# Register loads of TensorE from a multiple of four words on, and one column value per tile in the flow stage

## The chip, the cores and the metric

The kernel runs on one core of a Trainium2 chip. The metric is the device time of one execution in microseconds (us); lower is better. A core has five engines that each follow their own instruction stream and meet through semaphores: TensorE (PE, matrix products), VectorE (DVE), ScalarE (ACT), GpSimd (POOL) and SyncE (SP). TensorE has a sequencer (shown as PEq or PEldq) that reads the stream, carries out register work itself and hands the matrix instructions on.

## The reference, cut to what matters

Four layers over a graph of 3125 nodes with 32 features and 53125 edges, each on a normalised `h` and added to `x`:

```python
h = relu(layernorm(x)); x = x + relational(relational(h))   # twice: sum over edges of a message by source and edge type
h = relu(layernorm(x)); x = x + segment_sum(h[src], dst, N) # sum layer
h = relu(layernorm(x)); x = x + flow(h, src, dst, edge_attr) # small MLP per edge, summed forward and backward
h = relu(layernorm(x)); x = x + attention(h, src, dst)       # softmax over the edges of a node, 4 heads
```

Each layer needs, for every edge, a row of its source node, and adds a result to the sum of its destination node.

## The kernel before

The edges are first sorted by block of destination: a node block holds 128 nodes (`NB` = 25 blocks), and every tile of 128 edges has destinations in one block only. There are `T` = 440 tiles. The sums of all nodes lie in PSUM as 25 column ranges of 32, so to add a tile, TensorE multiplies a one-hot of the destinations with the messages and writes to columns `col` to `col` + 32, where `col` is the tile's block times 32. These 440 column values lie as int32 words in one row of SBUF, `dst_columns` (`s["dcol"]`); TensorE's sequencer loads them into registers with `pe.load`, and `pe.snap` makes a value of a register that an address can use.

**Relational stages (rel1, rel2; `add_up_pass`).** A group is 11 tiles, 40 groups a stage. For 8 tiles of a group, POOL gathers the message rows with 8 indirect DMAs (L726, six buffers). For the other 3 tiles TensorE picks the source rows itself: DVE makes one-hots of the sources, one 128x384 comparison for each of the 25 blocks (L789, two buffers `which`), and TensorE runs 25 matmuls over them (`pick`, L863). Per group TensorE's stream is: `pick(g)`, `gathered_messages(g)` (8 sums, which wait for POOL's DMAs), `coefficients(g)`, `picked_messages(g-2)`, `basis_products(g)`. `pick(g)` begins with the load of the group's 11 column values (L858), and behind it in the stream comes the wait for `which_ready`.

**Sum stage (`sum_layer`).** Again 11 tiles a group and 40 groups; 7 tiles are gathered by POOL (L1029, four buffers), 4 are picked (25 comparisons of 128x512 at L1063, 25 matmuls at L1115). The load is L1110, at the head of `pick`; the order is `pick(g+1)`, `turn(g)`, `picked_rows(g-1)`, `gathered_rows(g)`.

**Flow stage (`flow_layer`).** A group is 4 tiles, 110 groups. `pick_destinations` loads 4 column values (L1379) and runs 12 small matmuls that read at the column; `add_up`, two groups later, runs 12 sums into the column and 24 into the backward accumulator. The two are interleaved by `step`. Each use calls `col(b, t)`, which snaps the register again (L1369). The attention stage has its own load of 8 words (L1767).

SP brings in the source rows; ACT moves picked results from PSUM to SBUF.

Of the kernel before, what the change touches and what calls it, by code (L numbers as in the profile page):

```python
# [19 lines left out]
F = 32  # L20
# [5 lines left out]
NB = (N + P - 1) // P  # L26
# [8 lines left out]
G = 8  # L35
# [35 lines left out]
def stages(rounds):  # L71

    def stage(function, i, k, behind, *more):
        i, k = i + (k - behind) // BUFS, (k - behind) % BUFS
        if not isinstance(i, int) or 0 <= i < rounds:
            function(i, i * BUFS + k, k, *more)
    return stage

def top(x):
# [543 lines left out]
RG, RPT, RBUFS = 11, 3, 6  # L625
# [48 lines left out]
def add_up_pass(nc, a, s, d, sb, ps, sem, k, init, finish):  # L674
# [3 lines left out]
    name = f"rel{k}"  # L678
    with ExitStack() as st:
        acc = ps(st, f"{name}_acc", [P, 2 * BANK])  # L680
        parts = init(st, acc)
        with ExitStack() as st1:
# [28 lines left out]
            with nc.Block() as block:  # L711
# [133 lines left out]
                @block.tensor  # L845
                def _(pe):
                    if k == 1:
                        edges["pe"](pe)
                    parts["pe"](pe)
                    regs = [[pe.alloc_register(f"{name}_col{i}{t}") for t in range(RG)] for i in range(3)]  # L850

                    def add(g, t, rhs):
                        col = pe.snap(regs[g % 3][t], min_val=0, max_val=(NB - 1) * F)
                        return pe.matmul(acc[:, bass.ds(col, F)], hot[g % RBUFS][:, t, :], rhs,
                                         start=False, stop=True, skip_group_check=True)

                    def pick(g):
                        pe.load(regs[g % 3], s["dcol"][0:1, 0, g * RG:(g + 1) * RG])  # L858
                        pe.wait_ge(which_ready, g + 1)
                        if g >= 2:  # L860
                            pe.wait_ge(pick_taken, g - 1)
                        for c in range(NB):
                            last = pe.matmul(pp[g % 2][0:3 * F, 0:RW], hs[:, c].rearrange("p k f -> p (k f)"),  # L863
                                             which[g % 2][:, c, :], start=(c == 0), stop=(c == NB - 1))
                        last.then_inc(pick_done, 1)

                    def gathered_messages(g):
                        b = g % RBUFS
                        pe.wait_ge(hot_ready, g + 1)
                        pe.wait_ge(gathered[b], 16 * RGT * (g // RBUFS) + 16 * RGT)  # L870
                        for t in range(RGT):
                            last = add(g, t, rows[b][:, t, :])
                        last.then_inc(rows_used, 1)

                    def coefficients(g):
                        pe.wait_ge(kinds_ready, g + 1)
                        if g >= 1:
                            pe.wait_ge(coef_taken, g)
                        for t in range(RPT):
                            last = pe.matmul(pc[:, t * NBASIS:(t + 1) * NBASIS], kinds[g % 2][:, t * P:(t + 1) * P],  # L880
                                             ab[:], start=True, stop=True)
                        last.then_inc(coef_done, 1)

                    def basis_products(g):
                        pe.wait_ge(pick_taken, g + 1)
                        if g >= 1:
                            pe.wait_ge(z_taken, g)
                        for t in range(RPT):
                            for j in range(3):
                                last = pe.matmul(pz[:, t * NBASIS * F:(t + 1) * NBASIS * F],  # L890
                                                 gT[g % 2][:, t * P:(t + 1) * P], top(V[:])[:, j, :],
                                                 start=(j == 0), stop=(j == 2))
                        last.then_inc(z_done, 1)

                    def picked_messages(g):
                        pe.wait_ge(msg_ready, g + 1)
                        for t in range(RPT):
                            last = add(g, RGT + t, msg[g % 2][:, t, :])
                        last.then_inc(used, 1)

                    for g in range(RGROUPS):
                        pick(g)
                        gathered_messages(g)
                        coefficients(g)
                        if g >= 2:
                            picked_messages(g - 2)
                        basis_products(g)
                    picked_messages(RGROUPS - 2)
                    picked_messages(RGROUPS - 1)
# [79 lines left out]
def sum_layer(nc, a, s, d, sb, ps, sem, more):  # L989
# [3 lines left out]
    G, PT, bufs = 11, 4, 4  # L993
# [3 lines left out]
    with ExitStack() as st:  # L997
# [5 lines left out]
        with ExitStack() as st2:  # L1003
# [16 lines left out]
            with nc.Block() as block:  # L1020
# [76 lines left out]
                def _(pe):  # L1097
                    pe.wait_ge(zeroed, 2)
                    clear_acc(pe, s, zeros, [acc[:, 0:BANK], acc[:, BANK:2 * BANK]])
                    regs = [[pe.alloc_register(f"sum_col{i}{t}") for t in range(G)] for i in range(3)]  # L1100

                    def add(g, t, hot, rhs):
                        col = pe.snap(regs[g % 3][t], min_val=0, max_val=(NB - 1) * F)
# [3 lines left out]
                        return last  # L1107

                    def pick(g):
                        pe.load(regs[g % 3], s["dcol"][0:1, 0, g * G:(g + 1) * G])  # L1110
                        pe.wait_ge(which_ready, g + 1)
                        if g >= 2:
                            pe.wait_ge(pick_taken, g - 1)
                        for c in range(NB):
                            last = pe.matmul(pp[g % 2][0:3 * F, 0:PT * P], hs[:, c].rearrange("p k f -> p (k f)"),  # L1115
                                             which[g % 2][:, c, :], start=(c == 0), stop=(c == NB - 1))
                        last.then_inc(pick_done, 1)
# [116 lines left out]
def flow_layer(nc, a, s, d, sb, ps, sem, front):  # L1234

    G = 4
    rounds = T // G // BUFS
    stage = stages(rounds)
    with ExitStack() as st:  # L1240
# [6 lines left out]
        with ExitStack() as st2:  # L1247
# [22 lines left out]
            with nc.Block() as block:  # L1270
# [94 lines left out]
                def _(pe):  # L1365
                    regs = [[pe.alloc_register(f"flow_col{b}{t}") for t in range(G)] for b in range(BUFS)]

                    def col(b, t):
                        return pe.snap(regs[b][t], min_val=0, max_val=(NB - 1) * F)  # L1369

                    def turn_onehots(i, g, b):
                        pe.wait_ge(hot_ready, g + 1)
# [4 lines left out]
                    def pick_destinations(i, g, b, products):  # L1377
                        if products[0] == 0:
                            pe.load(regs[b], s["dcol"][0:1, 0, bass.ds(g * G, G)])  # L1379
                            pe.wait_ge(ot_copied, g + 1)  # L1380
                        for n in products:
                            t, k = divmod(n, 3)
                            last = pe.matmul(pQ[:, t * F:(t + 1) * F], OT[:, t, :],
                                             top(hpart[:])[:, k, bass.ds(col(b, t), F)], start=(k == 0), stop=(k == 2))
                        if products[-1] == 3 * G - 1:
                            last.then_inc(q_done, 1)

# [20 lines left out]
                    def add_up(i, g, b, products):  # L1408
                        if products[0] == 0:
                            pe.wait_ge(msg_ready, g + 1)  # L1410
                        for n in products:
                            t, k = divmod(n, 3)
                            pe.matmul(accF[:, bass.ds(col(b, t), F)], hot[b][:, t, :], top(M[b][:])[:, k, t, 0:F],  # L1413
                                      start=False, stop=True, skip_group_check=True)
                            for lo, hi in ((0, BANK), (BANK, QJ)):
                                last = pe.matmul(accB[:, lo:hi], S[b][:, t, k, :],  # L1416
# [534 lines left out]
```

## Time and profile before

| | us |
|---|---|
| median of 3 runs | 3631.74 (3630.74 to 3633.47) |
| profiled execution, span of its records | 3621.4 |
| rel1, first to last register load of its groups | 648.3 to 1075.0 |
| rel2, the same | 1164.3 to 1597.2 |
| sum, the same | 1632.7 to 2010.4 |
| flow, the same | 2040.9 to 2856.3 |

The stages follow each other, with a barrier of all engines between them: what a stage gains moves all later ones. PE is busy 72% of the span, DVE 71%, POOL 62%; which of them sets the pace differs from stage to stage. All times below count from the start of the span. The median lies 10.3 us above the span; the difference is taken as fixed.

### The profile page before, as it was taken

What the parts mean: (1) busy time and instruction counts of PE and PEld (TensorE: products, weight loads), DVE (VectorE), ACT (ScalarE), POOL (GpSimd) and SP (SyncE); (2) the same over time, 40 slices, a digit from 0 to 9 for tenths busy, and PEclk for the clock granted to TensorE, in tenths of its full rate; (3) what the DMA queues carried; (4) which work ended last, traced back from release to release, by engine and by line L of the source; (5) the groups of instructions that cost most, each with busy time, mean ns of one, the idle gap of its engine ahead of it and who ended that gap; (6) DMA issues with size and microseconds to landing.
All of it is one profiled execution on the core that took longest, in us unless ns stands there. A gap on an engine that the chain in (4) does not pass through costs nothing. (4 is left out here: it accounts for less than half of the span.)

```text
span 3621.4 us, 58407 instructions
## 1 busy us (share of the span) xinstructions
PE 2609.3 (72%) x19499; PEld 1755.0 (48%) x19499; DVE 2555.5 (71%) x7445; ACT 577.7 (16%) x1352; POOL 2259.7 (62%) x2253
## 2 busy tenths in 40 slices
PE   0600000999998999977889799999999967777751
PEld 0400000777776777764555466666666543333331
DVE  9400000998874988869999677777777559999987
ACT  0100000000001000000011122222222213333320
POOL 2777776877762777747777355555555357777750
PEclk9555555788885888878889799999999968888885
DMA  6300001111113111111111100000000011111120
GB/s 96 103 8 8 8 8 58 31 23 24 25 12 103 25 23 24 24 17 28 26 27 26 12 10 10 11 10 10 10 11 10 6 24 27 27 27 27 27 19 5
DMA packets 125028, 91.67 MB, mean 25 GB/s; under 512 B 59542, under 2 KB 110678, under 8 KB 124118
## 3 DMA queue, kind: packets, MB, share of 16 engines
q0 software_dynamic: 70912, 41.10, 7.7%
q1 hardware_dynamic: 53846, 46.89, 5.3%
q8 instruction: 178, 2.92, 0.3%
q14 instruction: 92, 0.75, 0.1%
HBM read 60.42 MB, written 27.41 MB: 24 GB/s over the span
## 5 line engine op out<-in xcount | busy, mean ns | idle before, releaser
L726 POOL DMA_INDIRECT rel_rows<-message_table,message_indices x640 | 684.8, 1070 | 285.3 <-issue 193.9
L1279 POOL DMA_INDIRECT flow_x<-node_table,flow_index x440 | 441.0, 1002 | 409.8 <-DVE flow_index L1294 300.8
L1416 PE MATMUL flow_acc_bwd<-flow_onehot_j,flow_by_q 128*128 128x512 bf16 x2640 | 573.2, 336 | 0.0
L789 DVE TENSOR_SCALAR rel_source_onehot<-rel_sources,node_numbers 128x384 bf16<-128x384 f16 x2000 | 511.1, 320 | 79.4 <-PE p_rel_picked L863 78.0
L387 POOL DMA_INDIRECT sorted_edges<-stage,sorted_row x416 | 405.0, 974 | 192.0 <-issue 126.6
L863 PE MATMUL p_rel_picked<-rel_source_onehot,rel_h_parts 128*96 128x384 bf16 x2000 | 483.2, 417 | 53.7 <-issue 53.3
L1644 POOL DMA_INDIRECT att_kv_rows<-kv_table,att_index x440 | 427.1, 971 | 141.1 <-issue 131.7
L863 PEld LDWEIGHTS p_rel_picked<-rel_source_onehot,rel_h_parts 128*96 128x96 bf16 x2000 | 315.0, 161 | 214.2 <-issue 69.7
L1029 POOL DMA_INDIRECT sum_rows<-node_table,src_indices x280 | 272.1, 972 | 103.1 <-issue 80.8
L658 PE MATMUL p_rel_terms<-ident,source_centred 128*128 128x128 f32 (+1 forms) x4 | 1.1, 434 | 454.4 <-DVE source_centred L644 454.4
L1063 DVE TENSOR_SCALAR sum_source_onehot<-sum_sources,node_numbers 128x512 bf16<-128x512 f16 x1000 | 305.6, 371 | 14.9 <-PE p_sum_picked L1115 14.7
L755 DVE COPY p_rel_lanes<-iota 128x128 f32<-128x128 f32 x2 | 0.6, 294 | 438.8 <-PEq L382 436.2
L1680 DVE TENSOR_REDUCE att_tile_max<-p_att_scores 128x4 f32<-128x512 f32 x440 | 284.3, 685 | 28.0 <-PE p_att_scores L1794 23.1
L1115 PE MATMUL p_sum_picked<-sum_source_onehot,sum_h_stack 128*96 128x512 bf16 x1000 | 257.7, 421 | 51.4 <-issue 40.0
L1792 PE MATMUL p_att_scores<-att_mask,identb 128*128 128x512 bf16 x440 | 201.4, 458 | 67.2 <-ACT att_parts_turned L1728 67.2
L1413 PE MATMUL flow_acc_fwd<-flow_messages,flow_onehot 128*128 128x32 bf16 x1320 | 234.8, 178 | 1.4 <-DVE flow_by_q L1322 1.4
L838 ACT CAST rel_picked<-p_rel_picked 96x384 bf16<-96x384 f32 x80 | 38.0, 475 | 1171.6 <-PE p_rel_picked L863 1171.6
L658 PEld LDWEIGHTS p_rel_terms<-ident,source_centred 128*128 128x128 f32 (+1 forms) x4 | 0.7, 202 | 455.8 <-DVE source_centred L644 455.8
L1307 DVE TENSOR_TENSOR flow_messages<-p_hidden,flow_b 128x256 f32<-128x256 f32 x110 | 46.7, 425 | 245.9 <-PE p_hidden L1404 245.9
L1115 PEld LDWEIGHTS p_sum_picked<-sum_source_onehot,sum_h_stack 128*96 128x96 bf16 x1000 | 133.4, 137 | 162.6 <-issue 80.6
L1322 DVE TENSOR_TENSOR flow_by_q<-flow_messages,source_q_mask 128x512 bf16<-128x512 bf16 x330 | 207.4, 682 | 0.0
L1794 PE MATMUL p_att_scores<-att_parts_turned,att_pick 96*128 96x512 bf16 x440 | 205.7, 467 | 0.0
(286 smaller groups left out, 4882.9 us busy)
## 6 DMA issues: line engine op xcount, KB each, us to landing
message_table<-message_rows SPq DMA_DIRECT2D x50, 320.0 KB, 2.2
rel_rows<-message_table,message_indices POOLq DMA_INDIRECT x640, 2.5
rel_sources<-source_rows SPq DMA_DIRECT2D x80, 96.0 KB
flow_x<-node_table,flow_index POOLq DMA_INDIRECT x440
att_kv_rows<-kv_table,att_index POOLq DMA_INDIRECT x440, 2.4
sorted_edges<-stage,sorted_row POOLq DMA_INDIRECT x416
sum_sources<-source_rows SPq DMA_DIRECT2D x40, 128.0 KB, 3.0
sum_rows<-node_table,src_indices POOLq DMA_INDIRECT x280, 2.3
```

The lines of the kernel that those rows point to most:

```text
L387: pool.indirect_dma_start(out=d["sorted"], out_offset=bass.IndirectOffsetOnAxis(ap=row[:, c:c + 1], axis=0), in_=stage[:, c, :], in_offset ...
L726: pool.indirect_dma_start(out=rows[b][:, t, :], out_offset=None, in_=d["messages"], in_offset=bass.IndirectOffsetOnAxis(ap=s["idx_msg"][:, ...
L789: last = dve.tensor_scalar(which[g % 2][:, c, :], srcs[b][:], s["node"][:, c:c + 1], None, ALU.is_equal)
L863: last = pe.matmul(pp[g % 2][0:3 * F, 0:RW], hs[:, c].rearrange("p k f -> p (k f)"), which[g % 2][:, c, :], start=(c == 0), stop=(c == NB ...
L1029: pool.indirect_dma_start(out=rows[b][:, t, :], out_offset=None, in_=d["nodes"], in_offset=bass.IndirectOffsetOnAxis(ap=s["idx_src"][:, g ...
L1063: last = dve.tensor_scalar(which[g % 2][:, c, :], srcs[g % bufs][:], node[:, c:c + 1], None, ALU.is_equal)
L1115: last = pe.matmul(pp[g % 2][0:3 * F, 0:PT * P], hs[:, c].rearrange("p k f -> p (k f)"), which[g % 2][:, c, :], start=(c == 0), stop=(c == ...
L1279: pool.indirect_dma_start(out=X[b][:, t, 0:F], out_offset=None, in_=d["nodes"], in_offset=bass.IndirectOffsetOnAxis(ap=ibuf[b][:, t:t + 1] ...
L1413: pe.matmul(accF[:, bass.ds(col(b, t), F)], hot[b][:, t, :], top(M[b][:])[:, k, t, 0:F], start=False, stop=True, skip_group_check=True)
L1416: last = pe.matmul(accB[:, lo:hi], S[b][:, t, k, :], J[b][:, t, lo:hi], start=False, stop=True, skip_group_check=True)
L1644: pool.indirect_dma_start(out=KV[b][:, t, :], out_offset=None, in_=d["kv"], in_offset=bass.IndirectOffsetOnAxis(ap=ibuf[b][:, t:t + 1], ax ...
L1680: dve.tensor_reduce(tm[b][:, 0, t, :], pR[t % PR][:].rearrange("p (h e) -> p h e", h=HEADS), AX_X, ALU.max).then_inc(max_ready, 1)
```

## The change

A helper begins a load at the multiple of four words at or below the first word wanted; the 0 to 3 words ahead of it go into registers that nobody reads. It is used in the two relational stages and the sum stage, where a group's first word is 11g, so that the remainder of 4 runs 0, 3, 2, 1 and the lengths are 11, 14, 13, 12 words. In flow the snap is made once per tile, at the first of its three picks, and the value is kept in a dictionary for the other two picks and the three sums. No array operation is added or removed, and the other engines' streams are the same.

```diff
+def load_aligned(eng, unused, regs, table, first):
+
+    before = first % 4
+    eng.load(unused[0:before] + regs, table[:, first - before:first + len(regs)])
...
                     regs = [[pe.alloc_register(f"{name}_col{i}{t}") for t in range(RG)] for i in range(3)]
+                    unused = [pe.alloc_register(f"{name}_unused{i}") for i in range(3)]
...
-                        pe.load(regs[g % 3], s["dcol"][0:1, 0, g * RG:(g + 1) * RG])
+                        load_aligned(pe, unused, regs[g % 3], s["dcol"][0:1, 0, :], g * RG)
...
                     regs = [[pe.alloc_register(f"sum_col{i}{t}") for t in range(G)] for i in range(3)]
+                    unused = [pe.alloc_register(f"sum_unused{i}") for i in range(3)]
...
-                        pe.load(regs[g % 3], s["dcol"][0:1, 0, g * G:(g + 1) * G])
+                        load_aligned(pe, unused, regs[g % 3], s["dcol"][0:1, 0, :], g * G)
...
-                    def col(b, t):
-                        return pe.snap(regs[b][t], min_val=0, max_val=(NB - 1) * F)
+                    cols = {}
...
                             t, k = divmod(n, 3)
+                            if k == 0:
+                                cols[b, t] = pe.snap(regs[b][t], min_val=0, max_val=(NB - 1) * F)
                             last = pe.matmul(pQ[:, t * F:(t + 1) * F], OT[:, t, :],
-                                             top(hpart[:])[:, k, bass.ds(col(b, t), F)], start=(k == 0), stop=(k == 2))
+                                             top(hpart[:])[:, k, bass.ds(cols[b, t], F)], start=(k == 0), stop=(k == 2))
...
-                            pe.matmul(accF[:, bass.ds(col(b, t), F)], hot[b][:, t, :], top(M[b][:])[:, k, t, 0:F],
+                            pe.matmul(accF[:, bass.ds(cols[b, t], F)], hot[b][:, t, :], top(M[b][:])[:, k, t, 0:F],
                                       start=False, stop=True, skip_group_check=True)
```

```order
127 L890 MATMUL p_rel1_terms<-rel1_basis_parts,rel1_picked1 128x256 x8
128 L858 TENSOR_LOAD dst_columns
129 L863 MATMUL p_rel1_picked0<-rel1_source_onehot0,rel1_h_parts 96x384 [waits rel1_pick_taken,rel1_source_onehot_ready]
130 L863 MATMUL p_rel1_picked0<-rel1_source_onehot0,rel1_h_parts 96x384 x24
131 L853 ISA [waits rel1_moved2,rel1_onehot_ready]
```

And after:

```order
127 L897 MATMUL p_rel1_terms<-rel1_basis_parts,rel1_picked1 128x256 x8
128 L84 TENSOR_LOAD dst_columns
129 L870 MATMUL p_rel1_picked0<-rel1_source_onehot0,rel1_h_parts 96x384 [waits rel1_pick_taken,rel1_source_onehot_ready]
130 L870 MATMUL p_rel1_picked0<-rel1_source_onehot0,rel1_h_parts 96x384 x24
131 L860 ISA [waits rel1_moved2,rel1_onehot_ready]
```

Nothing moved: it is still one load in the same place, of another start and length, which these rows don't print.

TensorE's stream in the flow stage, where picks of one group are interleaved with sums of an earlier one, before:

```order
3721 L1379 TENSOR_LOAD dst_columns
3722 L1369 ISA [waits message_copied10]
3723 L1383 MATMUL p_dst_rows<-flow_h_parts,flow_onehot_turned 128x32
3724 L1369 ISA
3725 L1383 MATMUL p_dst_rows<-flow_h_parts,flow_onehot_turned 128x32
3726 L1369 ISA
3727 L1413 MATMUL flow_acc_fwd<-flow_messages1,flow_onehot1 128x32
3728 L1416 MATMUL flow_acc_bwd<-flow_onehot_j1,flow_by_q1 128x512
3729 L1416 MATMUL flow_acc_bwd<-flow_onehot_j1,flow_by_q1 128x309
```

And after:

```order
3711 L1386 TENSOR_LOAD dst_columns
3712 L1391 ISA [waits message_copied10]
3713 L1392 MATMUL p_dst_rows<-flow_h_parts,flow_onehot_turned 128x32
3714 L1392 ISA
3715 L1392 MATMUL p_dst_rows<-flow_h_parts,flow_onehot_turned 128x32
3716 L1422 MATMUL flow_acc_fwd<-flow_messages1,flow_onehot1 128x32
3717 L1425 MATMUL flow_acc_bwd<-flow_onehot_j1,flow_by_q1 128x512
3718 L1425 MATMUL flow_acc_bwd<-flow_onehot_j1,flow_by_q1 128x309
```

The picks keep one ISA each; of the sums only the first of a tile keeps one. Over the stage 2640 ISA become 1760 (24 a group become 16).

## Rows read from the trace of the kernel before

**Rows 1.** The page: span, and one row of its DMA issues (us to landing).

```profile
span 3621.4 us, 58407 instructions
...
rel_rows<-message_table,message_indices POOLq DMA_INDIRECT x640, 2.5
```

**Rows 2.** Register loads by line: duration ns min/median/max, first and last start.

```profile
L1379 PEldq TENSOR_LOAD <-dst_columns x110: 329/333/347, 2040.9 to 2856.3; - x110
L858 PEldq TENSOR_LOAD <-dst_columns x80: 1317/2633/2669, 648.3 to 1597.2; - x80
L1767 PEldq TENSOR_LOAD <-dst_columns x55: 587/591/601, 2939.9 to 3496.1; - x55
L1110 PEldq TENSOR_LOAD <-dst_columns x40: 1316/2632/2657, 1632.7 to 2010.4; - x40
```

**Rows 3.** The same view for two single loads of rel2, groups 4 and 5.

```profile
L858 PEldq TENSOR_LOAD <-dst_columns x1: 1317/1317/1317, 1208.8 to 1208.8; - x1
L858 PEldq TENSOR_LOAD <-dst_columns x1: 2637/2637/2637, 1218.8 to 1218.8; - x1
```

**Rows 4.** Windows, from load to load, rel2 groups 4 to 7: stretch, length, busy times, PEclk.

```profile
1208.79:1218.80 10.01, 10.01 (x64) 8.07 (x63) 9.87 (x32) 0.65 (x2) 7.57 (x9) 0.83 0.17 24
1218.80:1231.13 12.33, 11.34 (x64) 8.55 (x63) 9.78 (x33) 0.66 (x2) 9.59 (x10) 0.72 0.13 23
...
sum 44.32, PE 41.45 PEld 32.45 DVE 39.46 ACT 2.62 POOL 34.26; mean PE 10.36 PEld 8.11 DVE 9.86 ACT 0.65 POOL 8.57
```

**Rows 5.** Waits in rel2, 1208.79 to 1563.70, 32 groups: us in total, times, longest.

```profile
PE p_rel_picked L863 <- issue: 22.7, 24, 1.0
```

**Rows 6.** Windows cut at POOL's groups of 8 DMAs (PE, PEld, DVE, ACT, POOL busy).

```profile
712.10:746.40 34.30, 33.39 (x202) 25.72 (x200) 34.30 (x114) 1.96 (x6) 27.05 (x24) 0.80 0.13 23
746.50:1069.70 323.20, 302.45 (x1803) 236.11 (x1802) 287.00 (x935) 18.98 (x58) 250.22 (x240) 0.81 0.14 22
960.30:1069.70 109.40, 101.85 (x607) 79.41 (x606) 96.09 (x319) 6.54 (x20) 85.14 (x80) 0.80 0.15 18
1179.80:1214.50 34.70, 32.87 (x193) 25.35 (x192) 34.60 (x115) 1.97 (x6) 27.60 (x24) 0.81 0.12 23
1225.90:1588.30 362.40, 339.38 (x2034) 265.30 (x2032) 321.35 (x1043) 21.60 (x66) 279.71 (x272) 0.81 0.14 22
1485.70:1588.30 102.60, 95.61 (x568) 74.30 (x566) 91.39 (x295) 5.89 (x18) 78.37 (x80) 0.80 0.15 18
```

**Rows 7.** Timeline of rel2, one DMA issue of POOL and DVE beside it.

```profile
1235.34 1.31 POOL L726 DMA_INDIRECT rel_rows<-message_table,message_indices  x1 [0.30 <-issue]
...
1235.30 1.23 DVE L789 TENSOR_SCALAR rel_source_onehot<-rel_sources,node_numbers 128x384 bf16<-128x384 f16 x5
```

**Rows 8.** Timeline: POOL's last gather and TensorE's sums over it, rel1 and rel2.

```profile
1068.55 1.08 POOL L726 DMA_INDIRECT rel_rows<-message_table,message_indices  x1 [0.30 <-issue]
...
1083.25 1.87 PE L854 MATMUL rel_acc<-rel_rows,rel_onehot 128*128 128x32 f32 x16
...
1586.92 1.30 POOL L726 DMA_INDIRECT rel_rows<-message_table,message_indices  x1 [0.31 <-issue]
...
1605.49 1.76 PE L854 MATMUL rel_acc<-rel_rows,rel_onehot 128*128 128x32 f32 x15
```

**Rows 9.** Sum stage: four groups from 1870.60 (windows), DVE's waits 1632 to 2012, end (timeline).

```profile
sum 37.56, PE 33.19 PEld 21.82 DVE 36.35 ACT 3.85 POOL 27.68; mean PE 8.30 PEld 5.46 DVE 9.09 ACT 0.96 POOL 6.92
...
DVE sum_source_onehot L1063 <- PE p_sum_picked L1115: 14.7, 13, 3.0
...
2008.00 1.40 DVE L1063 TENSOR_SCALAR sum_source_onehot<-sum_sources,node_numbers 128x512 bf16<-128x512 f16 x5
...
2013.21 3.01 PE L1115 MATMUL p_sum_picked<-sum_source_onehot,sum_h_stack 128*96 128x512 bf16 x7 [1.39 <-issue]
```

**Rows 10.** Flow: 2060 to 2860 (windows), and the snaps' register work, ns.

```profile
2060.00:2860.00 800.00, 798.04 (x7106) 513.93 (x7105) 569.26 (x1715) 232.47 (x536) 428.89 (x428) 1.00 0.06 10
...
L1369 PEldq FUSED_REGOPS  x2640: 44/56/73, 2043.4 to 2871.3; - x189
```

## The prediction, made before the changed kernel ran

> **What bounds the kernel now.** I read the register loads first, since the change is about them. Their time depends on where they begin, not on how many registers they fill: 4 words from a multiple of four take 333 ns, 8 words 591 ns, but 11 words take either 1.32 or 2.63 us [rows 2]. The trace gives both for the same line: group 4 of rel2 starts at word 44 and takes 1317 ns, group 5 starts at word 55 and takes 2637 ns [rows 3]; one group in four is of the first kind. So four words cost 591 - 333 = 258 ns, and the three words left over in an aligned load of 11 cost (1320 - 591) / 3 = 243 ns each, as much as each of the 11 words of an unaligned one (2633 / 11 = 239). An aligned load reads four words at a time, an unaligned one word by word.
>
> Then the windows from load to load: does the load hold up the array? In group 4 of rel2 PE is busy for all of 10.01 us, in group 5 for 11.34 of 12.33 us [rows 4], and the waits confirm it: 24 times in 32 groups PE stood idle before the pick with nothing to wait for but its own sequencer, 22.7 us in all, 0.95 each [rows 5]. The sequencer runs ahead of the array by the other 1.7 us (2.63 - 0.95). In the sum stage the idle time before a pick is 1.39 us [rows 9], so there it runs only 1.25 us ahead, plus what is too short to be listed.
>
> Last, who comes next. Four groups take 44.32 us in rel2, 11.08 each, with PE busy 10.36 of that, DVE 9.86, POOL 8.57 [rows 4]. POOL looks idle a quarter of the time, but it isn't free: between two of its DMA instructions lie 0.30 us of "issue" that nothing else ends [rows 7], and its 8 instructions with these gaps took 323.20 / 30 = 10.77 us a group in rel1 and 362.40 / 34 = 10.66 in rel2 [rows 6]. It is nearly as late as PE.
>
> **Part 1: shorter loads.** By the prices above the new loads take: 11 words 1.32 us as now; 14 words 333 + 2 x 258 + 2 x 243 = 1.34; 13 words 333 + 516 + 243 = 1.09; 12 words 0.85. That removes 9.22 - 4.60 = 4.62 us of sequencer time in four groups. All four are below 1.7 us, so in rel nothing of them is left in PE's idle time; in the sum stage 1.34 is at the edge of the cover, where I count 0.1 us in one group of four, 1 us in all at most. PE's idle time removed is 0.95 x 3 in four groups of rel (60 groups, 57 us) and 1.39 x 3 in sum (30 groups, 42 us). That would be 99 us if PE alone set the pace; it doesn't.
>
> **Rel: POOL takes over.** The last gather of rel1 is issued at 1068.55 and lands 2.5 us later [rows 1, 8], at 1071.1; PE adds it at 1083.25. In rel2 it lands at 1586.9 + 2.5 = 1589.4, and PE adds it at 1605.49 [rows 8]. PE's queue order puts these sums behind the pick; with PE free of the loads they wait for the DMA. So rel1 can gain 12.2 us and rel2 16.1 as long as POOL keeps its pace. POOL has six buffers and waits for nobody, but its pace depends on DVE: while DVE runs a row of five comparisons, a DMA instruction takes 1.31 us instead of 250.22 / 240 = 1.04 on average [rows 6, 7], and where DVE was busy all the time POOL's group took 34.30 / 3 = 11.43 and 34.70 / 3 = 11.57 us [rows 6]. DVE, less held up by PE, will be busier. I draw a line between the two kinds of stretch (period 9.9 us: POOL 11.5; period 11.08: POOL 10.7) and look where POOL's pace is the period: 10.7 + 0.67 (11.08 - p) = p gives p = 10.85. Against 10.77 over 30 groups that is 2.4 us later in rel1, against 10.66 over 34 groups 6.5 us in rel2. Gains: 12.2 - 2.4 = **9.8**, and 16.1 - 6.5 = **9.6**. PE's own 10.36 fits in 10.85, so it is not the bound. The extremes of POOL's pace at today's period are 109.40 / 10 = 10.94 and 102.60 / 10 = 10.26 [rows 6]. With about 11.1 (the first, and a little for the busier DVE) the two gains are 12.2 - 30 x 0.33 = 2 and 16.1 - 34 x 0.44 = 1; with 10.26 POOL is ahead of PE, and PE's 10.36 sets the pace.
>
> The port behind this has a page: the Trainium skill, "SBUF — State Buffer", section "Who interferes with whom", says that DVE in a two-port mode and GpSimd lock each other out for whole instructions. The trace agrees that POOL's instruction is stretched beside the comparisons [rows 7]; by a full lock whenever DVE compares, rel would gain nothing, which is the second rival's case.
>
> **Sum: DVE takes over.** DVE is busy 9.09 us a group and PE 8.30 of 9.39 [rows 9]. All that DVE waits for in the stage is 14.7 us, for picks [rows 9]. Its last comparison ends near 2009.4, and the last pick starts at 2013.21 [rows 9], 3.8 us later, because PE is behind. If DVE never waits and the pick follows at once, the gain is 14.7 + 3.8 = 18.5 us. It waits for single picks up to 3.0 us, where TensorE's clock was low, and that can't go wholly; the 1 us above comes off as well. I take **16**, bounds 8 (half of the waits stay) and 18.5. POOL is not near in this stage: its 7 instructions and gaps are 6.92 + 7 x 0.30 = 9.0 us of 9.39 [rows 9], and DVE keeps the period at 9.1.
>
> **Part 2: kept column values in flow: nothing.** Eight of 24 register instructions a group go, 8 x 56 ns = 0.45 us of the sequencer, 49 us in 110 groups [rows 10]. But PE is busy 798.04 of 800.00 us there at full clock (1.00, that is 2.4 GHz) [rows 10]: the array is fed without a gap, the sequencer's work lies wholly beneath it, and less of it changes nothing. Bounds: nothing lost, and the 2.0 us of idle as the most to win. The load of 4 words there was aligned before.
>
> Sum: 9.8 + 9.6 + 16 = 35.4 us. Span 3621.4 - 35.4 = 3586.0; median 3631.7 - 35.4 = **3596.3 us**, 0.97% faster.
>
> **Rivals.**
> 1. *POOL quick, PE the bound in rel.* With PE at 10.36 instead of 11.08 over the 30 and 34 groups rel gains 22 and 24 us, with sum's 18.5 in all 65: 3567. For it: POOL did 10.26 for ten groups. Against it: POOL's rows with a busy DVE. Chance 0.11.
> 2. *POOL slow.* Rel gains 2 + 1, sum 14: 17 us, 3615. For it: 11.43 and 11.57 beside a busy DVE; against it, a slow POOL holds up PE, hence DVE, and then speeds up itself. Chance 0.17.
> 3. *The waits move but the time doesn't.* TensorE's clock falls in each group now (0.83 and 0.72 [rows 4]); if in sum PE, waiting for DVE, is at 1.2 GHz for longer, its pick takes the place of the load, and together with rival 2 it leaves less than 7 us: 3628. Chance 0.05.
> 4. *Slower: the wider load is no faster.* If reading by fours needs more than the start (the unused registers stand apart from the others), the loads go word by word: 14, 13 and 12 words at 239 ns are 3.35, 3.11 and 2.87 us, 1.44 us more in four groups than 3 x 2.63. The cover is used up, so all of it is idle time of PE, in the 20 sets of four of rel and 10 of sum: 43 us, 3675. It decides from a load above 2.63 us on. Against it: aligned loads of three different register sets all took 1.32 us. Chance 0.05. The Trainium skill, "Runtime: NRT & Kernel Launch", section "Instruction fetch mechanics", has such a rule: about 200 ns a register even in bulk, which would make 12.5 words on average 0.3 us dearer than 11, 36 us in 120 loads. It speaks of loads from HBM; the trace disagrees for SBUF, with 591 ns for 8 registers [rows 2].
>
> **How the numbers follow.** The forecast has 0.62. Its own gain runs from 20 to 46 us. To leave out no more than 2 in 10, the range takes in rival 2 and part of rival 1: 3580 to 3616. A measurement of this kernel can tell about 0.2% (7.3 us) from no change; faster by more are the forecast and rivals 1 and 2, 0.90; rival 3 is the same, 0.05; rival 4 slower, 0.05.
>
> **What would show it.** The loads, now on the helper's line, at 0.85 to 1.34 us, none above; no idle time of PE "issue" before picks in rel; in its place waits of the gathered sums for the DMA of rel_rows, with POOL's groups at 10.8 to 10.9 us; in sum, PE waiting before picks for DVE's comparisons and DVE idle for less than 3 us; flow the same length to 2 us. A load above 1.7 us, a POOL pace outside 10.4 to 11.1, or DVE waits in sum above 7 us would make it wrong.

## The result, and the profile after

| | median us | lowest to highest | runs |
|---|---|---|---|
| before | 3631.24 | 3630.13 to 3633.47 | 4 |
| after | 3606.02 | 3605.05 to 3613.36 | 4 |

The changed kernel takes 0.9933 of the time, with an interval of 0.9919 to 0.9947: 25.2 us less, where 35.4 had been forecast (3596.3 us). The time lies in the range, and faster was right. But the stages don't add up as forecast. In this table (us) a stage runs from its first register load to the first one of the next. The row "after, forecast" is before plus the terms of the prediction.

```
                 to rel1    rel1    rel2     sum    flow    rest     span
before             648.3   515.9   468.4   408.2   899.0   681.5   3621.4
after, forecast            506.1   458.8   392.2   899.0           3586.0
after              647.7   525.8   476.5   382.8   891.8   679.1   3603.6
```

Sum gained 25.4 us instead of 16. Rel, which should have gained 9.8 and 9.6, is 9.9 and 8.1 us longer in this execution. Flow's 7.2 us come up again below.

First the loads. In the view of the instructions of one tile (duration ns lowest/median/highest, first and last start), the first three rows are rel1, rel2 and sum, the fourth is one load of 14 words, the last is flow:

```profile
L84 PEldq TENSOR_LOAD <-dst_columns x40: 850/1212/1517, 647.7 to 1079.0; - x40
...
L84 PEldq TENSOR_LOAD <-dst_columns x40: 852/1208/1345, 1173.5 to 1607.7; - x40
...
L84 PEldq TENSOR_LOAD <-dst_columns x40: 852/1212/1345, 1650.0 to 2005.1; - x40
...
L84 PEldq TENSOR_LOAD <-dst_columns x1: 1345/1345/1345, 881.6 to 881.6; - x1
...
L1386 PEldq TENSOR_LOAD <-dst_columns x110: 329/334/341, 2032.8 to 2848.2; - x110
```

None is near the 2.63 us of [rows 2]. The single load of 1345 ns is that of rel1's group 21, of 14 words; the lowest values of 850 ns are loads of 12 words. The 1517 ns is the very first load of rel1, of 11 words; no later one in these stages takes more than 1358.

Next the waits of the changed kernel over the whole span (us in total, times, longest):

```profile
PE rel_acc L861 <- DMA rel_rows<-message_table,message_indices: 53.9, 28, 4.3
...
PE p_sum_picked L1123 <- DVE sum_source_onehot L1070: 33.9, 25, 7.9
...
DVE rel_source_onehot L795 <- PE p_rel_picked L870: 61.4, 35, 3.9
```

and of the kernel before:

```profile
PE p_rel_picked L863 <- issue: 53.3, 59, 1.0
...
PE p_sum_picked L1115 <- issue: 40.0, 28, 1.5
...
DVE rel_source_onehot L789 <- PE p_rel_picked L863: 78.0, 53, 2.8
```

The idle time of TensorE on its own sequencer before these picks is gone (0.2 us is left in sum), as it should be. In rel 53.9 us of waits for gathered rows stand in the place of 53.3: a full exchange. In sum 33.9 stand in the place of 40.0, and there the time fell. So the load was removed from TensorE's path in both stages, and only in one of them did the time follow.

Windows (stretch, length, busy us of PE, PEld, DVE, ACT and POOL, granted TensorE clock as a share of 2.4 GHz, DMA share, GB/s) of sum, rel2 and flow in the changed kernel:

```profile
1685.90:1988.20 302.30, 280.26 (x1874) 184.55 (x1873) 302.30 (x987) 32.61 (x68) 229.77 (x238) 0.93 0.18 29
...
1250.00:1500.00 250.00, 237.74 (x1409) 190.59 (x1409) 224.87 (x734) 14.61 (x46) 195.38 (x180) 0.81 0.15 23
...
2051.00:2848.00 797.00, 786.59 (x6933) 511.66 (x7065) 566.94 (x1707) 231.92 (x535) 431.77 (x428) 1.00 0.08 10
```

In the sum stage VectorE is busy 302.30 of 302.30 us over 34 groups, 8.89 us each: it is now the bound, without a gap. In rel2 no engine is: PE has 12 us idle in 250, DVE 25. POOL's 180 DMA instructions with 0.30 us between them make 195.38 + 54 = 249.4 of the 250 us: POOL is never free. That alone doesn't make it the bound, since it gathers ahead into six buffers; Experiment 2 is the test. In flow PE is nearly full as before; some of its matmul records are missing in this row.

### The profile page after: what moved, and what is told of

Its sections match the earlier page's. It is cut to its first block and busy times, and to the rows that moved or that the text cites. A ratio compares the mean times of both kernels' runs of the same rounds, so it can differ in the third digit from the quotient of the medians.

```text
span 3603.6 us, 57390 instructions
## 1 busy us (share of the span) xinstructions
PE 2602.2 (72%) x19362; PEld 1786.6 (50%) x19499; DVE 2548.7 (71%) x7445; ACT 576.6 (16%) x1352; POOL 2289.0 (64%) x2253
## 5 line engine op out<-in xcount | busy, mean ns | idle before, releaser
L732 POOL DMA_INDIRECT rel_rows<-message_table,message_indices x640 | 716.3, 1119 | 279.2 <-issue 194.4
L1425 PE MATMUL flow_acc_bwd<-flow_onehot_j,flow_by_q 128*128 128x309 bf16 (+1 forms) x2503 | 552.2, 334 | 8.9 <-issue 0.2
L870 PE MATMUL p_rel_picked<-rel_source_onehot,rel_h_parts 128*96 128x384 bf16 x2000 | 429.4, 384 | 0.4 <-DVE rel_source_onehot L795 0.4
L870 PEld LDWEIGHTS p_rel_picked<-rel_source_onehot,rel_h_parts 128*96 128x96 bf16 x2000 | 297.0, 149 | 122.1 <-issue 0.7
L1123 PE MATMUL p_sum_picked<-sum_source_onehot,sum_h_stack 128*96 128x512 bf16 x1000 | 250.5, 413 | 34.5 <-DVE sum_source_onehot L1070 33.9
L861 PE MATMUL rel_acc<-rel_rows,rel_onehot 128*128 128x32 f32 x1280 | 166.3, 287 | 54.2 <-DMA rel_rows<-message_table,message_indices 53.9
```

The lines of the kernel that those rows point to most:

```text
L732: pool.indirect_dma_start(out=rows[b][:, t, :], out_offset=None, in_=d["messages"], in_offset=bass.IndirectOffsetOnAxis(ap=s["idx_msg"][:, ...
L1425: last = pe.matmul(accB[:, lo:hi], S[b][:, t, k, :], J[b][:, t, lo:hi], start=False, stop=True, skip_group_check=True)
```

## Experiment 1: each part alone

The edits put two of the three places back to the code before. In `e1_rel_only` only the loads of rel are aligned; sum's load and flow's columns are as before:

```
-                        load_aligned(pe, unused, regs[g % 3], s["dcol"][0:1, 0, :], g * G)
+                        pe.load(regs[g % 3], s["dcol"][0:1, 0, g * G:(g + 1) * G])
...
-                    cols = {}
+                    def col(b, t):
+                        return pe.snap(regs[b][t], min_val=0, max_val=(NB - 1) * F)
```

> Aligned loads in the two relational stages alone; sum and flow as before. Theory A (POOL's gathers take over the pace of rel, and a busier DVE stretches them): total within 8 us of before, in its profile PE's idle time before picks gone and as much again in waits for the gathered rows; rel not shorter than before. Theory B (rel does gain, and the profile of the changed kernel caught an unlucky execution): 8 to 20 us faster than before.

In `e2_sum_only` rel's load is put back instead of sum's (flow as before too), and in `e3_flow_only` both loads are put back and only flow's kept column values stay:

```
-                        load_aligned(pe, unused, regs[g % 3], s["dcol"][0:1, 0, :], g * RG)
+                        pe.load(regs[g % 3], s["dcol"][0:1, 0, g * RG:(g + 1) * RG])
```

> Aligned loads in the sum stage alone. Theory A: the whole gain of the change is here, 23 to 28 us faster than before, with the sum stage at DVE's own 8.89 us a group. Theory B: about 15 us, the rest of the change's gain is rel's.

> One column value per tile in flow alone, all loads as before. Both theories: no change, within 3 us, since TensorE's array is busy 99.8% of the flow stage. A third one, that the 49 us of register work saved were partly in the open, would give 5 us or more.

`e4_after_again` is the changed kernel once more, on the same chip.

> The changed kernel again, for a closer time and a second profile. Both theories: 22 to 28 us faster than before. If the longer rel stages of its first profile (459 and 461 us against 448 and 453) are of the kernel, they are there again; if of one execution, rel1 and rel2 come out within 3 us of before's.

Measured:

| kernel | median us (runs) | ratio to before, 95% interval |
|---|---|---|
| rel's loads alone | 3630.83 (12) | 1.0013 (0.9998 to 1.0027) |
| sum's loads alone | 3604.20 (6) | 0.9939 (0.9925 to 0.9952) |
| flow's columns alone | 3629.55 (12) | 1.0006 (0.9996 to 1.0016) |
| all, again | 3604.00 (6) | 0.9933 (0.9917 to 0.9948) |

The whole gain is sum's. Rel's loads and flow's columns are worth nothing that can be measured. The stages of the profiled executions say the same: sum takes 385.4 and 384.3 us where its load is aligned, and 404.9 and 411.6 where it isn't. Rel1 and rel2 together take 989.7 and 994.8 us with the old loads and 1006.2 and 992.3 with the aligned ones, against 984.3 and 1002.3 in the first two profiles. One execution's rel part differs by 10 to 14 us from another's of the same code, so the 18 us that rel lost between the first two profiles are not a price of the change. The mean of the three pairs is 10.7 us, and the interval of the run with rel's loads alone allows a loss of 10 us at most and a gain of 1.

What rel's aligned loads did is seen in the waits of `e1_rel_only` and `e2_sum_only`:

```profile
PE rel_acc L861 <- DMA rel_rows<-message_table,message_indices: 55.2, 32, 4.5
...
PE p_sum_picked L1122 <- issue: 39.8, 28, 1.5
```

```profile
PE p_rel_picked L869 <- issue: 56.2, 60, 1.0
...
PE p_sum_picked L1122 <- DVE sum_source_onehot L1069: 32.1, 25, 7.9
```

Each exchange belongs to its own stage, and neither needs the other part. But the old loads don't always hide POOL: in the profile of `e3_flow_only`, whose rel stages are those of before, TensorE waits for gathered rows too:

```profile
PE rel_acc L860 <- DMA rel_rows<-message_table,message_indices: 6.3, 4, 3.3
```

The POOL instructions themselves became longer with the aligned loads. Here are the groups of the costliest instructions (count, busy us, mean ns, idle time before them) of the changed kernel, of `e1_rel_only` and of `e2_sum_only`. The mean is 1070 ns in the kernel before and 1095 in `e3_flow_only`, and 1106 in `e4_after_again`: 1032 to 1095 with the old loads, 1106 to 1126 with the aligned ones.

```profile
L732 POOL DMA_INDIRECT rel_rows<-message_table,message_indices x640 | 716.3, 1119 | 279.2 <-issue 194.4
```

```profile
L732 POOL DMA_INDIRECT rel_rows<-message_table,message_indices x640 | 720.5, 1126 | 281.8 <-issue 194.5
```

```profile
L732 POOL DMA_INDIRECT rel_rows<-message_table,message_indices x640 | 660.2, 1032 | 312.8 <-issue 194.2
```

## Experiment 2: relieve POOL in rel

If POOL is the bound of rel after the change, less work for POOL must give in the changed kernel what it doesn't give in the old one. Both kernels of this pair gather seven of a group's eight tiles of rows; the eighth tile's sums add the seventh's rows once more, so TensorE and VectorE do the same work as ever and the values of that tile are left out. `e6_after_7` is the changed kernel with this, `e7_before_7` the kernel before with it.

```
-                        for t in range(RGT):
+                        for t in range(RGT - 1):
...
-                            pe.wait_ge(gathered[b], 16 * RGT * (g // RBUFS) + 16 * RGT)
+                            pe.wait_ge(gathered[b], 16 * (RGT - 1) * (g // RBUFS) + 16 * (RGT - 1))
...
-                            last = add(g, t, rows[b][:, t, :])
+                            last = add(g, t, rows[b][:, min(t, RGT - 2), :])
```

> The changed kernel, with 7 instead of 8 gathers per group in rel; the eighth tile adds the seventh's rows again, so the sums are of other rows, and TensorE's and DVE's work is the same. Theory A (POOL sets rel's pace after the change): with 1.25 us less of POOL a group, rel falls to DVE's 9.9 to PE's 10.4 us a group, 50 to 90 us less over the two stages than the changed kernel, some 3530 us in all. Theory C (rel stands still for another reason, PE's low clock or DVE's waits): within 15 us of the changed kernel.

> The kernel before with the same 7 gathers, the sums being of other rows. If PE with its unaligned loads set rel's pace at 11.08 us, a POOL that is 1.25 us shorter changes little: 0 to 15 us faster than before. If POOL was already the bound before the change, it gains as much as the changed kernel does, 50 us or more.

Measured: after with seven gathers 3548.34 us, 0.9780 of before (0.9753 to 0.9806); before with seven gathers 3628.17, 0.9983 (0.9965 to 1.0000). With the old loads an eighth less work on POOL is worth some 6 us; with the aligned ones some 56 more than the change itself. Rel1 and rel2 take 494.4 and 439.9 us in the one and 520.0 and 468.4 in the other. The waits between 1250 and 1500 us, first of `e6_after_7`, then of `e7_before_7`:

```profile
PE rel_acc L861 <- DMA rel_rows<-message_table,message_indices: 6.7, 7, 1.5
```

```profile
PE p_rel_picked L863 <- issue: 16.1, 17, 1.0
...
POOL rel_rows L726 <- PE rel_acc L854: 5.8, 5, 2.5
```

In the second, TensorE is back at its own loads, and POOL runs into the six buffers and waits for TensorE's sums. So the kernel before was bound by TensorE with its loads in rel, the changed one is bound by POOL.

## Experiment 3: where POOL's time goes

Why did POOL become slower, when nothing of its own was changed? One held-up stretch of rel1 in the timeline of the changed kernel (start, us, instruction, count): POOL's DMA instructions first, VectorE's beside them, then TensorE's.

```profile
830.80 1.04 POOL L732 DMA_INDIRECT rel_rows<-message_table,message_indices  x1 [0.30 <-issue]
832.14 2.42 POOL L732 DMA_INDIRECT rel_rows<-message_table,message_indices  x1 [0.30 <-issue]
834.87 2.96 POOL L732 DMA_INDIRECT rel_rows<-message_table,message_indices  x1 [0.30 <-issue]
838.14 0.94 POOL L732 DMA_INDIRECT rel_rows<-message_table,message_indices  x1 [0.30 <-issue]
...
832.88 0.54 DVE L782 TENSOR_TENSOR rel_onehot<-p_rel_lanes,dst_in_block 128x384 f32<-128x384 f32 x1
833.35 1.27 DVE L795 TENSOR_SCALAR rel_source_onehot<-rel_sources,node_numbers 128x384 bf16<-128x384 f16 x5
834.55 0.53 DVE L782 TENSOR_TENSOR rel_onehot<-p_rel_lanes,dst_in_block 128x384 f32<-128x384 f32 x1
...
836.15 0.54 DVE L782 TENSOR_TENSOR rel_onehot<-p_rel_lanes,dst_in_block 128x384 f32<-128x384 f32 x1
836.62 1.27 DVE L795 TENSOR_SCALAR rel_source_onehot<-rel_sources,node_numbers 128x384 bf16<-128x384 f16 x5
837.81 0.93 DVE L812 TENSOR_TENSOR rel_terms<-p_rel_terms,rel_coef 128x768 f32<-128x768 f32 x1
...
843.33 3.00 PE L861 MATMUL rel_acc<-rel_rows,rel_onehot 128*128 128x32 f32 x16 [3.44 <-DMA rel_rows<-message_table,message_indices]
```

Two instructions of POOL, of 0.94 us when undisturbed, take 2.42 and 2.96 us. They end at 834.56 and 837.83, each time just as VectorE's run of five comparisons is over and a TENSOR_TENSOR starts. Neither got through at the end of the run before: a whole TENSOR_TENSOR (from 832.88 and from 836.15, 0.54 us each) lies inside each. Some microseconds later TensorE stands still for 3.44 us for those rows. Such instructions (over 1.7 us) are 31 of 640 in the changed kernel; counted in its trace, all 31 span exactly one such break between two runs of comparisons, and 27 end within 0.06 us of the end of a run. There are 35 and 34 of them in `e1_rel_only` and `e4_after_again`, and 14, 9 and 28 with the old loads (before, `e2_sum_only`, `e3_flow_only`). They are about half of what POOL loses: all that the changed kernel's 640 instructions take beyond 0.94 us each is 115 us, of which these 31 have 53. The rest is instructions of 1.0 to 1.7 us.

If the long rows of comparisons hold POOL up, the same work in another order frees it. In rel VectorE makes a group's 25 comparisons in 5 runs of 5, with 4 pieces of the 11 tiles' one-hot product (2 or 3 tiles each) between them. `e8_runs8` makes 8 runs of 3 or 4 with 7 pieces, `e11_runs10` 10 runs of 2 or 3 with 9 pieces, `e9_runs12` 12 runs (eleven of 2, one of 3) with 11 pieces of one tile each. All of them are the changed kernel otherwise. `e10_before_runs12` is the same order of 12 runs in the kernel before, with the old loads. The edit, with 12:

```
+RUNS = 12
...
-                        for n in range(FIFTHS):
-                            sources(g, n * NB // FIFTHS, (n + 1) * NB // FIFTHS)
-                            if n < FIFTHS - 1:
-                                onehots(g, n * RG // (FIFTHS - 1), (n + 1) * RG // (FIFTHS - 1))
+                        for n in range(RUNS):
+                            sources(g, n * NB // RUNS, (n + 1) * NB // RUNS)
+                            if n < RUNS - 1:
+                                onehots(g, n * RG // (RUNS - 1), (n + 1) * RG // (RUNS - 1))
```

> The changed kernel, DVE's comparisons in rel in 8 runs of 3 or 4 between 7 pieces of destination one-hots, instead of 5 runs of 5 between 4. If POOL is held up by runs of comparisons and let in between them, there are fewer of its 2.4 to 3.0 us instructions, at 0.2 us more of DVE a group: 10 to 40 us faster than the changed kernel. If it is held up by the number of comparisons whatever their order, no gain, or up to 10 us slower.

> The same with 12 runs of 2 or 3 comparisons between 11 pieces of one tile each, at 0.5 us more of DVE a group (to 10.4). By the first reading 10 to 40 us faster than the changed kernel, perhaps less than with 8 runs as DVE becomes the bound; by the second 0 to 20 us slower.

> The kernel before, with 12 runs of comparisons in rel and its word-by-word loads in all stages. Theory A (rel has two bounds of nearly the same height, the loads in PE's path and POOL's stretched gathers, and only both together move it): rel stays at PE's 11.08 us a group, within 12 us of before, while with aligned loads the same order gave 83 us less. Theory D (the finer runs alone do it, the loads have no part in rel): 50 us or more faster than before.

> The changed kernel with 10 runs, 9 one-hot pieces: 0.13 us less of DVE a group than with 12 runs, 10.7 us over both stages, but runs of 2 to 3 comparisons that come less often apart. If DVE, busy 247.8 of 250 us with 12 runs, is the bound and POOL is already free, 3538 to 3546 us; if POOL is still stretched with pieces of more than one tile, 3550 to 3585.

Measured:

| kernel | median us | ratio to before, 95% interval | rel1 + rel2 us | POOL's mean ns |
|---|---|---|---|---|
| after (5 runs), again | 3604.00 | 0.9933 (0.9917 to 0.9948) | 992.3 | 1106 |
| after, 8 runs | 3588.08 | 0.9892 (0.9862 to 0.9922) | 964.0 | 1060 |
| after, 10 runs | 3577.97 | 0.9854 (0.9837 to 0.9870) | 961.6 | 1062 |
| after, 12 runs | 3547.72 | 0.9771 (0.9745 to 0.9797) | 933.8 | 1011 |
| before, 12 runs | 3629.23 | 0.9992 (0.9979 to 1.0005) | 990.9 | 1003 |

The windows from 1250 to 1500 us of 12 runs, 10 runs, and 12 runs with the old loads:

```profile
1250.00:1500.00 250.00, 244.60 (x1506) 195.62 (x1504) 247.83 (x958) 16.13 (x49) 192.00 (x190) 0.83 0.16 24
```

```profile
1250.00:1500.00 250.00, 242.07 (x1445) 192.34 (x1444) 233.91 (x860) 15.05 (x46) 192.85 (x188) 0.82 0.15 24
```

```profile
1250.00:1500.00 250.00, 234.18 (x1387) 182.56 (x1388) 226.73 (x878) 14.35 (x44) 191.80 (x192) 0.80 0.16 24
```

and the timeline of the 12 runs kernel, POOL's instructions beside VectorE's alternation of two comparisons and one piece:

```profile
1299.58 1.01 POOL L733 DMA_INDIRECT rel_rows<-message_table,message_indices  x1 [0.30 <-issue]
1300.90 1.02 POOL L733 DMA_INDIRECT rel_rows<-message_table,message_indices  x1 [0.30 <-issue]
...
1299.71 0.53 DVE L796 TENSOR_SCALAR rel_source_onehot<-rel_sources,node_numbers 128x384 bf16<-128x384 f16 x2
1300.17 0.27 DVE L783 TENSOR_TENSOR rel_onehot<-p_rel_lanes,dst_in_block 128x128 f32<-128x128 f32 x1
```

This order costs VectorE more instructions and more time: 247.83 us busy of 250 against 224.87, for 24.5 groups there instead of 22.9. POOL's instructions are near 1.01 us in this stretch, beside a VectorE that is never idle; 2 of 640 are over 1.7 us. The gain over the changed kernel is 56 us by the two medians and 59 by the two ratios, more than the 10 to 40 expected. No engine is the only bound now: PE has 5.4 us idle in 250, VectorE 2.2, and POOL's 190 instructions with their gaps fill 192.00 + 57 = 249 of the 250.

The last row of the table is the test from the other side. With the old loads POOL's mean falls from 1070 to 1003 ns and the time doesn't move, for TensorE stands idle on its loads as ever. POOL fills 191.80 + 58 of the 250 us here too, without being what sets the pace:

```profile
PE p_rel_picked L864 <- issue: 16.1, 17, 1.0
```

Short loads alone: 1.0013. Short runs alone: 0.9992. Both, sum's 22 to 25 us set aside: some 58 us. Rel had two bounds of nearly the same height, and each hid the other.

Between 10 and 12 runs what matters isn't settled: the 10 have five runs of three comparisons instead of one, and also two pieces of two tiles. It isn't the instructions over 1.7 us, of which the 10 have one: they have 156 of 1.2 to 1.4 us, the 12 have 21. And in every one of these orders the pieces between the runs get shorter with the runs; the two were never tried apart.

## Why the prediction was right in sum and wrong in rel

**The loads.** 1.34, 1.09, 0.85 and 1.32 us were worked out from three rows of before, and 1.34, 1.10, 0.855 and 1.32 measured. The fourth rival, that the wide load goes word by word, fell with them. So did, for loads from SBUF, the rule of about 200 ns a register that the prediction cites beside it from the Trainium skill, "Runtime: NRT & Kernel Launch", section "Instruction fetch mechanics": 12 words take 71 ns each. Nearly none of the idle time that the loads had made was left (0.2 us), as forecast.

**Rel: POOL takes over.** The step was right in kind, and its numbers were wrong. The prediction drew a line through two kinds of stretch (10.7 us a group at today's pace, 11.5 beside a full VectorE) and read 10.85 off it. POOL's pace from 1250 to 1500 us is 250 / 180 x 8 = 11.1 us, at the edge of what the prediction itself named as the sign of being wrong. That is the value of the second rival, which gave rel 2 + 1 us; the comparison of rel's loads alone allows a gain of 1 us at most and a loss of up to 10. The error is in treating the pace as a function of VectorE's load alone. An undisturbed instruction takes 0.94 us and a caught one up to 2.97, and how VectorE's work is ordered matters more than how busy it is: with VectorE at 247.83 of 250 us and short runs POOL's pace is 250 / 190 x 8 = 10.5 us a group, where the line, at its 10.2 us a group, would give 11.3 and where 30 groups of rel1 and 34 of rel2 had 10.77 and 10.66 before [rows 6]. The prediction took the stretch of a single instruction to be 1.31 us [rows 7]; of its two windows beside a full VectorE, the one of 11.43 us a group has nothing over 1.41 us but three instructions of 1.27 to 1.41 in each group, and that of 11.57 us has one of 2.83 [rows 6].

**Rel: the slack of the last gather.** A second term was mis-sized, and it is a reading of before. The prediction lets the last gather of each stage land 2.5 us after its start, which is the median of all 640 [rows 1]. The view of the last gather alone, rel2 of the kernel before (start 1586.9), then rel1 of the changed kernel (start 1083.8):

```profile
DMA to landing us min/median/max: 5.9/5.9/5.9
```

```profile
DMA to landing us min/median/max: 6.5/6.5/6.5
```

The gathers of rel2's last group land ever later, the first 3.5 us after its start and the eighth 5.9; why isn't shown. So rel2's last rows of before were there at 1592.8, 12.6 us ahead of their sum and not 16.1. For rel1 of before the trace has no landing; with the 5.6 to 6.5 us that it takes in rel1 of the other profiles the slack was 8.2 to 9.1 us instead of 12.2, an estimate. Put into the prediction's own sum with a pace of 11.1, the two gains are 8.6 - 9.9 = -1.3 and 12.6 - 15.0 = -2.4: rel had nothing to gain, which is what was measured. About 7 of the 19.4 us forecast for rel come from this term, the rest from the pace.

**Rel: the mechanism.** That runs of five comparisons with their pieces hold POOL is shown by the reordering. That they do it by a port which both use was not tried apart, nor does any run show in which mode the comparisons run; the page that the prediction cites, "SBUF — State Buffer" of the Trainium skill, section "Who interferes with whom", says it, and the ends of the two long instructions at 834.56 and 837.83 agree with it. Its whole-instruction lock beside every comparison doesn't show: with 12 runs POOL takes 1.01 us beside comparisons, 7% over the undisturbed 0.94.

**Sum: DVE takes over.** Right, and too small: 25.4 us here, and 25.1 as the difference of the means of all profiles (five with the old load, 404.9 to 411.6; seven with the new one, 382.8 to 385.6). The bound above was 18.5 = 14.7 of VectorE's waits and 3.8 of the pick's lag at the end. The lag went nearly as a whole: the last comparison ends at 2005.79 and the last pick starts at 2006.39, 0.6 us later.

```profile
2004.40 1.39 DVE L1070 TENSOR_SCALAR sum_source_onehot<-sum_sources,node_numbers 128x512 bf16<-128x512 f16 x5
...
2006.39 5.58 PE L1123 MATMUL p_sum_picked<-sum_source_onehot,sum_h_stack 128*96 128x512 bf16 x25
```

The waits went to zero, those for the low clock too, because PE at 8.2 us of 8.89 catches up. What the bound left out is VectorE's own work, which was taken as fixed at 9.09 us a group [rows 9]. The rows of the comparisons, before and after, between 1690 and 1990 us:

```profile
L1063 DVE TENSOR_SCALAR sum_source_onehot<-sum_sources,node_numbers 128x512 bf16<-128x512 f16 x789 | 241.3, 371 | 14.5 <-PE p_sum_picked L1115 14.4
```

```profile
L1070 DVE TENSOR_SCALAR sum_source_onehot<-sum_sources,node_numbers 128x512 bf16<-128x512 f16 x844 | 252.4, 365 | 0.0
```

A comparison takes 6 ns less, 25 of them 0.15 us a group, 6 us in 40 groups. 14.7 + 3.2 + 6 = 23.9 of the 25.1. Why a comparison got shorter isn't shown. It is not that those after a wait are longer: only 13 of the 1000 follow one, at 385 ns, and the others of before have 371 as well.

**Flow: nothing.** Right. The kept columns alone gave 1.0006 (0.9996 to 1.0016). The register work fell as described:

```profile
L1391 PEldq FUSED_REGOPS  x440: 68/68/73, 2035.3 to 2850.0; - x147
L1422 PEldq FUSED_REGOPS  x440: 37/42/42, 2050.2 to 2862.5; - x147
```

First load to last is 815.4 us after and 815.4 before [rows 2]. The 7.2 us of the table come later, between flow and the next stage, where TensorE's clock stayed at 2.4 GHz in this execution and fell to 1.2 in that of before. The windows of before, then of after:

```profile
2881.00:2895.70 14.70, 14.70 (x30) 3.94 (x29) 3.01 (x5) 3.41 (x5) 0.00 (x0) 0.50 0.00 0
```

```profile
2872.00:2881.00 9.00, 8.75 (x31) 2.94 (x31) 3.65 (x7) 3.75 (x6) 0.00 (x0) 1.00 0.00 0
```

In the profiles of `e2_sum_only` and `e4_after_again` the same part is at the low clock again, and in that of `e1_rel_only`, whose flow is that of before, it stays at the high one (flow 891.3 us in the count of the first table), so it goes with the execution and not with the change.

**The offset.** The prediction took the 10.3 us between the span of before and the median as fixed. They are not: each execution's time is 1.8 us above its own span. The profiled execution of before was just a quick one (3623.2 us); 23 executions of that kernel lie between 3616.9 and 3638.7 us. The offset drops out of the forecast as a difference. But POOL's pace and slack were read from this one execution, with 14 instructions over 1.7 us, where `e3_flow_only` has 28 in the same rel stages and TensorE waiting for gathered rows.

**The sum of it.** With rel's gain taken as nothing, 19.4 us too much for rel, 9 too little for sum, nothing in flow: 35.4 - 19.4 + 9 = 25. That the total came out as near as it did was luck: two errors of opposite sign.

## What to carry to other kernels

Where several engines are each nearly the bound, ask for each edit what is late next, and try the two edits together: here short loads and short comparison runs are worth nothing apart and 58 us as a pair. Load registers from a multiple of four words on, even if some registers are filled for nothing. And where POOL issues gathers, try not to let VectorE run many comparisons in a row, even if the shorter runs cost VectorE more instructions: here the order of VectorE's work stretched POOL's instructions more than its load did. Last, where a stage ends on a DMA, read the landing of that DMA and not the median of all.

## What the runs showed of the hardware

- A register load of TensorE from SBUF that starts at a multiple of four words takes 333 ns for the first four words, 258 for each further four and about 240 for each one left over; 11 words from another start take 2.63 us, 239 ns for every word. 14 registers in 1.34 us against 11 in 2.63.
- A POOL DMA instruction of 0.94 us was stretched to as much as 2.97 us beside runs of five comparisons on VectorE, past a TENSOR_TENSOR of 0.54 us between two runs, and to 1.01 beside runs of two with a TENSOR_TENSOR of 0.27 us between.
- The median gather lands 2.5 us after its start, the last of rel1 or rel2 5.6 to 6.5 us after, wherever the trace has it.
- The kernel's executions differ by 22 us (3616.9 to 3638.7, 23 of them) on the same code, in another 13 by 28 us (3618.7 to 3647.1), and rel's stages by 10 us or so from one profile to another. Since whether a POOL instruction is caught depends on how the two engines' instructions happen to lie, this is a likely source of it; it wasn't measured by itself.
